# A layernorm-attention-layernorm-FFN block on one core: the turn of the next batch's input moved from TensorE to VectorE blocks and DRAM, and the FFN's input left uncentred

## The reference, cut to what matters

```python
def reference(x, Wq, Wk, Wv, Wo, W, b, logits, u):
    def attn(x):
        q, k, v = x @ Wq, x @ Wk, x @ Wv
        s = where(causal, q @ k.T, -max)           # 1024 x 1024 per batch
        return softmax(s * 256 ** -0.5) @ v @ Wo
    def ffn(x):
        idx = argmax(log_softmax(logits) - log(-log(u)))   # one of 8 weights
        return x @ W[idx] + b[idx]
    x = x + layernorm(attn(layernorm(x)))
    return x + layernorm(ffn(layernorm(x)))        # layernorm: no gain, no offset, eps 1e-5
```

## Time and profile before

| what | us |
|---|---|
| median of 3 runs | 425.5 |
| lowest and highest run | 425.34, 428.11 |
| profiled execution, first to last instruction (its span) | 424.3 |
| median run less that span | 1.2 |
| TensorE busy in the span | 414.0 |
| VectorE, ScalarE, POOL busy | 339.8, 299.1, 118.3 |

### The profile page before, as it was taken

One profiled execution on the slowest core, in us unless ns is written; L12 is line 12 of the kernel. 1 busy time (PEld: TensorE's weight loads), 2 busy tenths in 40 slices (PEclk: granted clock), 3 DMA queues, 4 the chain that ended last, 5 costly groups with the idle time before them and its releaser, 6 DMA issues.

```text
span 424.3 us, 9812 instructions
## 1 busy us (share of the span) xinstructions
PE 414.0 (98%) x3045; PEld 393.2 (93%) x3045; DVE 339.8 (80%) x1010; ACT 299.1 (71%) x854; POOL 118.3 (28%) x237
## 2 busy tenths in 40 slices
PE   7999999999999999999999999999999999999993
PEld 7789999999999999999999999999999999999993
DVE  4578778987898878887788878898788887876776
ACT  5886877668766687568866687666885678756563
POOL 3103333232322232123421323223232224302133
PEclk9999999999999999999999999999999999999998
DMA  6310012110120101201021001201012000020003
GB/s 198 90 49 26 26 25 76 52 39 14 51 81 18 49 25 42 82 9 40 25 66 57 25 25 48 76 25 49 13 37 99 0 0 0 25 75 2 2 0 101
DMA packets 18951, 18.46 MB, mean 44 GB/s; under 512 B 1140, under 2 KB 18932, under 8 KB 18932
## 3 DMA queue, kind: packets, MB, share of 16 engines
q1 hardware_dynamic: 18660, 17.96, 13.5%
q10 hardware_dynamic: 272, 0.26, 0.2%
HBM read 9.83 MB, written 8.39 MB: 43 GB/s over the span
## 4 chain that ended last, share of the span: by engine, by line
PE 93%; DMA 2%; ACT 2%; DVE 1%; issue 0%; POOL 0%; SPq 0%; POOLq 0%; DVEq 0%
PE bank L805 54%; PE score L805 23%; PE bank L908 7%; PE bank L932 3%; PE bank L819 3%; DMA wq<-in_L_attn_Wq_dram 1%; DMA bias_raw<-in_L_ffn_b_dram 1%; PE score L891 1%; PE score L847 0%; PE bank L865 0%; POOL f_rstd L387 0%; PE score L835 0%; DVE out_sb L778 0%; ACT squares_junk L591 0%; ACT sums_junk L470 0%
## 5 line engine op out<-in xcount | busy, mean ns | idle before, releaser
L387 POOL TENSOR_TENSOR o_rstd<-o_ve,minus_half 128x1 f32<-128x1 f32 x64 | 35.2, 550 | 193.8 <-DVE o_ve L735 193.8
L805 PE MATMUL bank<-v_hi,pT_lo 128*128 128x256 f32 x288 | 84.6, 294 | 0.0
L805 PE MATMUL bank<-v_hi,pT_hi 128*128 128x256 f32 x288 | 81.4, 283 | 0.0
L805 PE MATMUL bank<-v_lo,pT_hi 128*128 128x256 f32 x288 | 81.3, 282 | 0.0
L805 PE MATMUL score<-xT_hi,g_lo 128*128 128x384 f32 (+4 forms) x176 | 63.7, 362 | 0.0
L805 PE MATMUL score<-xT_hi,g_hi 128*128 128x384 f32 (+4 forms) x176 | 61.1, 347 | 0.0
L805 PE MATMUL score<-xT_lo,g_hi 128*128 128x384 f32 (+4 forms) x176 | 61.1, 347 | 0.0
L549 ACT ACTIVATE probs<-neg_scores,neg_max 128x128 f32<-128x128 f32 (+3 forms) x64 | 49.7, 776 | 14.0 <-DVE neg_max L707 13.5
L805 PEld LDWEIGHTS bank<-v_lo,pT_hi 128*128 128x128 f32 x288 | 55.0, 191 | 0.4
L805 PEld LDWEIGHTS bank<-v_hi,pT_lo 128*128 128x128 f32 x288 | 54.9, 191 | 0.3
L805 PEld LDWEIGHTS bank<-v_hi,pT_hi 128*128 128x128 f32 x288 | 54.9, 191 | 0.0
(11 more groups left out here) (112 smaller groups left out, 1130.5 us busy)
## 6 DMA issues: line engine op xcount, KB each, us to landing
x_sb<-in_L_attn_x_dram SPq DMA_DIRECT2D x32, 256.0 KB, 2.7
out_dram<-out_sb SPq DMA_DIRECT2D x31, 256.0 KB, 2.1
wq<-in_L_attn_Wq_dram ACTq DMA_DIRECT2D x1, 256.0 KB, 4.1
wk<-in_L_attn_Wk_dram SPq DMA_DIRECT2D x1, 256.0 KB, 4.4
wv<-in_L_attn_Wv_dram SPq DMA_DIRECT2D x1, 256.0 KB, 4.2
wo_raw<-in_L_attn_Wo_dram SPq DMA_DIRECT2D x1, 256.0 KB, 4.5
wf_raw<-in_L_ffn_W_dram SPq DMA_DIRECT2D x1, 256.0 KB, 2.7
out_dram<-out_sb SPq DMA_DIRECT2D x2, 128.0 KB, 2.1
```

The source lines that it names most:

```text
L387: return nc.gpsimd.tensor_tensor(dst[:, n0:n1], ve[:, n0:n1], minus_half[:, n0:n1], ALU.pow)
L805: last = nc.tensor.matmul(dst, l, r, start=(i == 0), stop=(i == len(passes) - 1))
```

## The change

The diff, cut to its core (the four lists of the last batch lose only ACT's K steps; those of the first seven are below in full):

```diff
+    QUAD = 32
+    QUADS = PART // QUAD
+    RUN = KC * NT * QUAD
-    PE_ORDER = """S0 V0 S1 V1 T0 S2 T1 S3 O0 V2 T2 O1 S4 T3 V3 O2 S5 O3 T4 S6 T5 S7 X0 Y0 O4 T6 O5 T7 O6 X1 Y1
-        O7 F0 G0 Y2 X2 F1 X3 F2 Y3 G1 G2 F3 G3"""
...
+    PE_ORDER = """S0 S1 V0 V1 T0 S2 T1 V2 O0 S3 T2 S4 O1 V3 T3 O2 S5 O3 T4 S6 Y0 T5 S7 O4 T6 O5 F0 T7 O6 Y1 O7 G0 G1
+        Y2 Y3 F1 G2 F2 F3 G3"""
+    ACT_ORDER = """E0 V0 E1 T0 V1 H0 T1 V2 E2 O0 E3 H1 T2 O1 V3 T3 O2 H2 E4 H3 O3 T4 E5 Y0 T5 E6 O4 T6 E7 O5 T7 X0 X1
+        O6 F0 Y1 X2 O7 X3 G0 G1 Y2 Y3 G2 F1 F2 F3 G3"""
+    DVE_ORDER = """M0 M1 L0 V0 T0 V1 M2 L1 T1 V2 M3 L2 C0 B0 R0 M4 T2 C1 L3 C2 T3 R1 V3 B1 R2 B2 M5 C3 T4 R3 B3 Y0 M6
+        T5 N0 M7 C4 N1 R4 T6 C5 R5 F0 T7 C6 N2 R6 Y1 C7 R7 G0 U0 G1 Y2 Y3 Z0 F1 N3 U1 F2 F3 U2 Z1 G2
+        U3 Z2 G3 Z3"""
+    POOL_ORDER = """L0 L1 C0 L2 L3 C1 C2 C3 N0 C4 C5 X0 X1 C6 N1 C7 X2 N2 X3 U0 N3 U1 U2 U3"""
...
+            def turn_x(b):
+                sp.wait_ge(x_blk_ready, (b + 1) * NP)
+                sp.dma_start(x_kept.rearrange("p q r -> p (q r)"), x_blk[:, :]).then_inc(x_blk_kept, 16)
+                sp.wait_ge(x_blk_kept, (b + 1) * 16)
+                kept = x_kept.rearrange("(i a) q r -> q a i r", i=QUADS)
+                for q in range(QUADS):
+                    sp.dma_start(xT_raw[q * QUAD:(q + 1) * QUAD, :].rearrange("a (i r) -> a i r", i=QUADS), kept[q]
+                                 ).then_inc(x_raw_loaded, 16)
+
             def sequence(b):
-                for p in range(NP):
+                load_after(b, 0)
+                turn_x(b)
+                for p in range(1, NP):
                     load_after(b, p)
...
@@ gpsimd @@
+                    elif kind == "X":
+                        pool.wait_ge(x_hi_ready, b * 2 * KC + n + 1)
+                        c, k = n // KC, n % KC
+                        nc.gpsimd.tensor_tensor(split_block(xT_lo, c, k), raw_block(c, k),
+                                                split_block(xT_hi, c, k).bitcast(f32), ALU.subtract
+                                                ).then_inc(x_lo_ready, 1)
...
-                        scales(y_nm, y_ve, y_rstd, y_shift, t0, t1).then_inc(y_shift_ready, 1)
+                        rstd(y_rstd, y_ve, t0, t1).then_inc(y_rstd_ready, 1)
...
@@ scalar @@
                     elif kind == "X":
-                        x_hi(at("X", n), n)
+                        c, k = n // KC, n % KC
+                        if n == 0:
+                            act.wait_ge(x_raw_loaded, (b + 1) * QUADS * 16)
+                            act.wait_ge(scores_ready, (b + 1) * NT)
+                            for j in range(KC):
+                                nc.scalar.activation(xT_first[:, j, :].rearrange("p (i s) -> p i s", i=QUADS),
+                                                     raw_block(0, j)[:, 0], ACT.Identity)
+                        nc.scalar.activation(split_block(xT_hi, c, k), raw_block(c, k),
+                                             ACT.Identity).then_inc(x_hi_ready, 1)
...
-                    elif kind == "K":
...
@@ vector @@
+            def x_blocks(b, p, first):
+                dve.wait_ge(xn_ready, b * NP + p + 1)
+                if not first:
+                    dve.wait_ge(x_blk_kept, (b - 1) * 16)
+                turned = x_blk[:, :].rearrange("p (q k t s) -> p t k q s", q=QUADS, k=KC, t=NT)
+                for t in (2 * p, 2 * p + 1):
+                    last = nc.vector.transpose(turned[:, t], xn[:, t, :].rearrange("p (k q a) -> p k q a", k=KC, q=QUADS))
+                last.then_inc(x_blk_ready, 1)
...
-                    elif kind == "X":
-                        x_lo(at("X", n), n)
...
-                        nc.vector.tensor_scalar(y_nm[:, t0:t1], y_mv[:, t0:t1, 0], -1.0, None, ALU.mult)
...
-                        nc.vector.tensor_tensor(f_sb[:, p, here, :],
-                                                cols(job.bank, (t1 - t0) * D).rearrange("p (t d) -> p t d", t=t1 - t0),
-                                                bias[:, None, :].broadcast_to([PART, t1 - t0, D]),
-                                                ALU.add).then_inc(bank_drained[job.bank], 1)
+                        dve.wait_ge(y_rstd_ready, b * NP + n + 1)
+                        for t in range(t0, t1):
+                            last = nc.vector.scalar_tensor_tensor(out=f_sb[:, p, t % 2, :],
+                                                                  in0=bank[job.bank][:, (t - t0) * D:(t - t0 + 1) * D],
+                                                                  scalar=y_rstd[:, t:t + 1], in1=bias[:, :],
+                                                                  op0=ALU.mult, op1=ALU.add)
...
@@ tensor @@
-                        pe.wait_ge(yn_ready, b * NP + n + 1)
-                        take_bank(job)
+                        take_bank(job, *(at("O", t) for t in range(t0, t1)))
...
-                                                       yn[:, p, t % 2, k * PART:(k + 1) * PART], ident[:, :])
+                                                       y[:, t, k * PART:(k + 1) * PART], ident[:, :])
-                    elif kind == "X":
-                        x_transposes(b + 1, at("X", n), n)
-                        g_quarter(at("G", n), [at("X", 2 * (n // 2) + 1)], n)
+                        g_quarter(at("G", n), [], n, turned=b)
```

More of the change, by code:

```diff
@@ L116, in jobs_of @@
                     yield (kind, n, g)
-            elif kind in "VOYFXGA":
+            elif kind in "VOYFGA" or kind == "X" and steps is BEFORE:
                 yield (kind, n, 0)
@@ L308, in cols, with raw_block, split_block @@
             return bank[bk][:, 0:n]
+        def raw_block(c, k):
+            cols_of = xT_raw[:, :].rearrange("p (i k t s) -> p k t i s", i=QUADS, k=KC, t=NT)
+            return cols_of[:, k, c * (NT // 2):(c + 1) * (NT // 2), :, :]
+        def split_block(half, c, k):
+            return half[:, k, c * BANK:(c + 1) * BANK].rearrange("p (t i s) -> p t i s", t=NT // 2, i=QUADS)
         def x_tile(b, t, n=1):
@@ L363, in _ @@
                 sequence(b)
+            turn_x(B - 2)
             for p in range(NP):
@@ L551, in sequence @@
                                              accum_out=exp_sums[:, n:n + 1]).then_inc(probs_ready, 1)
+                        if first and n == 3:
+                            ffn_weights(2)
                     elif kind == "T":
@@ L593, in sequence @@
                         last.then_inc(f_squares, 1)
-            sequence(0)
+            sequence(0, first=True)
             with act.Fori(1, B - 1) as b:
@@ L725, in sequence @@
                                                                                     t=t1 - t0))
-                    elif kind == "X":
-                        x_lo(at("X", n), n)
+                    elif kind == "B":
+                        x_blocks(b + 1, n, first=isinstance(b, int) and b == 0)
                     elif kind == "G":
@@ L821, in x_transposes, with g_quarter @@
                 last.then_inc(bank_full[job.bank], 1)
-            def g_quarter(job, inputs, n):
+            def g_quarter(job, inputs, n, turned=None):
                 c, m = n // 2, n % 2
+                if turned is not None:
+                    pe.wait_ge(x_lo_ready, turned * 2 * KC + (c + 1) * KC)
                 take_bank(job, *inputs)
@@ L886, in sequence @@
                             pe.wait_ge(bank_drained[g.bank], g.used + 1)
+                        if first and n == 2:
+                            pe.wait_ge(wf_centred, 1)
+                            for k in range(KC):
+                                means = nc.tensor.matmul(score[:, 1, 1, 0:D], averaging[:, :], wf[:, k, :], start=(k == 0),
+                                                         stop=(k == KC - 1))
+                            means.then_inc(wf_means_ready, 1)
+                        elif first and n == 5:
+                            pe.wait_ge(wf_twice_centred, 1)
                         h, w = pieces(n)
```

82 lines of the change are left out of this document (45 added, 37 removed).

## The result

| what | before | after |
|---|---|---|
| median of 20 runs, us | 425.92 | 427.44 |
| lowest and highest run, us | 425.34, 428.11 | 426.13, 430.66 |
| span of the profiled execution, us | 424.3 | 426.4 |
| one steady batch, S0 to S0, us | 49.92 | 49.74 |

The ratio is 1.0032, with a 95% interval from 1.002 to 1.0044: slower, within 1%, and outside the range of 413 to 422. All four X groups left TensorE, and a batch became 0.18 us shorter instead of 1.4.

The account below looks back on a forecast made before the run. TensorE's own work was taken as the bound; 424.3 - 12.3 (X groups) + 0.9 (averaging) + 2.1 (O2's wait) = 415.0 us of span, plus 1.2 for the median run, 416.2, said as 416. Range: 413 to 422.

Parts of the forecast that it names:

- What bounds: In the batches of the kernel before, TensorE's own work is the time, 49.92 us a batch, with no wait.
- What TensorE loses: Four X transpose groups of 0.44 us a batch leave TensorE's path, 12.3 us over seven batches.
- What TensorE gains: Two float32 averaging matmuls of 128x256, once, on the path in the first batch: 0.87 us.
- The other engines: Per batch: VectorE 43.6 of 48.16 us, ScalarE some 31.5, POOL about 18.5; transpose 0.415, POOL subtraction 1.2.
- First place: Batch's start on VectorE: M0 3.3 us after S0, slack used up; O2 waits 0.3 us a batch, 2.1 in all.
- Second place: DRAM round trip from B3 to X0: store 4.4, loads 5.0, 9.4 us in all, hidden up to 12.3 before G0.
- Third place: G2 waits for POOL's X3 behind C7, X2, N2; it fits by 0.6 us.
- The tail: Kernel's end goes over POOL's f_rstd and VectorE's Z, so Y4's earlier start gains 0.
- A: Rival: no wait anywhere, transposes cheap and M0 in time; 414.1 us, chance 0.15.
- B: Rival: VectorE bounds a batch's first half, transposes at 0.83; 426.7 us, no change; chance 0.15 including weaker forms.
- C: Rival: round trip ends late and G0 waits, costing from 12.3 us on; 435 at 15.3 us, chance 0.12.
- The sum: Profiled span 424.3 - 12.3 + 0.9 + 2.1 = 415.0 us; with 1.2 for the median run 416.2, said as 416.

Follow-up runs that it names:

- e0: Not a run: E0 is a step in ScalarE's list, following M0; it has no time of its own as a kernel.
- e2: Not a run and not named in the short version: E2 is a step in ScalarE's list, for which T2 waits.
- experiments 9 and 13: 9: changed kernel, POOL's C1 before L3, VectorE's T2 before M4, S0 before V0 in last batch, 421.58 us; 13: also V0 forward, H0 later, 420.32 us.
- experiment 4: Kernel before with only the second part: FFN weights centred over input rows too, y turned itself, X transposes still on TensorE; 428.59 us, ratio 1.0057.
- experiment 8: Changed kernel with the DRAM copy laid out so one load reaches all 128 partitions, store in four pieces of 32 partitions; 427.76 us, ratio 1.0045.
- experiment 7: Changed kernel with each VectorE block transpose done twice, first into a tensor nobody reads; 442.77 us, ratio 1.0384.

## Why the prediction was wrong, point by point

**What bounds.** Right for the kernel before. For the changed one the forecast was that TensorE stays the bound but for 0.3 us a batch; it waits 1.4.

**What TensorE loses.** Mis-sized: four groups at 0.44 taken from one row of the chain. Start to start the four are 1.59, not 1.76, since two of them stand where they cost 0.35; 11.1 us, not 12.3. A row was misread beside it: the 30 matmuls of the 5.62 us are one F and three G, not two and two; a G comes out at 1.4 either way.

**What TensorE gains.** 0.68 against 0.87. Right.

**The other engines.** Transpose, POOL's subtraction and F's two pieces came as forecast. The Trainium skill's rule in "GPSIMD Engine Reference", section on performance versus the Vector engine, agrees with this trace: 1.291 us for 512 elements against the estimate of 1.1 plus dispatch from it. VectorE has 42.44 us in 50, so 42.2 in a batch of 49.74, against 43.6 forecast. It is idle for 7.5 us a batch, but for only 1.5 of them before T3.

**First place.** This is the step that failed. M0 at 3.3 us after S0 is exact (178.06). O2's wait came as forecast (0.37 against 0.3), in part by luck: T2's low half is out 14.05 us after S0 and not 13.5, and the waits ahead of O2 make it due at 13.7 and not 13.2. But "the slack is used up, nothing more" is wrong, and only two chains were walked from M0: to T0, put at no wait where it waits 0.17, and over T2 to O2. Put at nothing without a look were three more: V2 waits for the bank of V0, whose low half stands behind L0 (0.23; the new TensorE list lets V2 take that bank 4.7 us after V0's start, where O0 took it after 6.4); through L3 POOL's C1 is late, and so R1 and O3 (0.34); and the fuller end of VectorE's list frees G2's bank late for V0 (0.13). O3's is the largest: I went through what stands behind POOL's X1 and X3, which are new steps, and not through L3, an old one that the new lists move. It stood behind C5 on both engines; now it is behind C1 on VectorE but ahead of C1 on POOL, and this crossing of the two orders could be read in the diff. The same holds for ScalarE's `E0 V0`, which was `V0 E0`. Over seven batches these four are 6.1 us.

**Second place.** The store took 3.9 us against 4.4, the loads 7.6 against 5.0. The runs decide for the rule that I had set beside my rates: the Trainium skill, "SBUF — State Buffer", section "Door 1: The DMA port swizzle", from which my estimate for the loads was 8.2. Hidden all the same, as forecast, but for batch 1 in this execution (1.15 us). 2.1 of the 2.9 us of slack went into it, and B3 ended 0.8 later than forecast; G0 itself is 1.2 later than forecast, by the waits ahead of it, so that POOL's X1 still ends 0.95 us ahead of it, where 1.5 was forecast.

**Third place.** G2 never waited in a steady batch. Right. **The tail.** The end itself gained nothing, as forecast; but the transition into the last batch, which has its own list with V0 first, cost 1.2 us, and the prediction did not look at it.

**Rivals.** A fell at once. B's size came (426.7 against 427.4), but not by its mechanism: the transposes run at 0.417, and experiments 9 and 13 make the kernel 5.9 and 7.1 us faster with every instruction of VectorE still in it; that the number fits is luck. C did not happen in a steady batch.

**The sum**, forecast to measured, in us: X groups 1.2 less gained; averaging 0.2 less lost; O2 0.5 more; O3 2.4; V0, T0 and T1 with V2 3.7; small ones 1.2; batch 1 1.15; the last transition 1.2. Together 11.1 of the 11.4 between the spans of 415.0 and 426.4; the rest lies in batches 0 and 2 and the last transition. Adding 1.2 us to the span was off as well: in the runs of the changed kernel each run's own span lies 1.8 to 1.9 below its time, so a span of 415.0 stood for some 416.8.

Open: what the remaining 0.4 us a batch between 48.33 (no wait) and 48.73 would need, most of it T0's and V0's wait for M0 and G2 at the batch's start; taking it away would need a step moved from one batch's list into the next, which was not tried. Open too are the late trip of batch 1 in some executions, and the late bias load in the head of experiment 4.

## What to carry to other kernels

When engines run fixed lists, an edit that delays one engine must be followed through every list that reads from it, old steps that only moved as much as new ones: ask of each step what stands behind it while it waits, and look for pairs of steps whose order differs between two engines. Where TensorE was the chain with no slack, removing work from it makes the next-latest of many near-ties visible, and several of them together cost more than any walk of one chain shows. And a wait that wanders when it is removed is no proof of an overloaded engine: look at whether it wanders behind the same step, as here H0, before calling it load.

## What was new about the hardware

- Loads from DRAM into 32 SBUF partitions moved 210 to 277 GB/s, one over all 128 partitions 342 to 387, in runs of 2 KB both and with the DMA engines over 90% busy in both cases: 7.6 against 5.6 us for 1 MB (the changed kernel and experiment 8). Stores out of 32 partitions took 6.0 us for 1 MB against 3.9 over 128, but in shorter runs as well.
- VectorE's 32x32 block transpose of 128x256 float32 takes 0.417 us, as much as reading the same elements once for statistics; a strided destination does not slow it (0.418 into a dense tensor, 0.403 into the strided one, experiment 7).
- A group of four 128x128 float32 transposes on TensorE costs 0.35 or 0.44 us, by the place where it stands.
